# Value blocks side by side behind an undivided fold, scores in the banks they free, and the high parts of a projection ahead of its low parts

## The chip, the cores and the metric

The kernel runs on one core of one Trainium2 chip. The metric is the device time of one execution in microseconds (us). The engines are TensorE (PE; its weight loads are listed apart as PEld), VectorE (DVE), ScalarE (ACT), GpSimd (POOL) and SyncE (SP, which only issues transfers here). PSUM has eight banks of 128 x 512 fp32 numbers, and TensorE writes nowhere else.

## The reference, cut to what matters

```python
h = einsum('bct,bcd->bdt', x, W[condition])          # x: 128 x 32 x 512, W[condition]: 32 x 32
q = (h @ Wq_c.T + bq_c) @ Wq_up.T + bq_up            # 32 heads of 192
kv = h @ Wkv_c.T + bkv_c                             # 64 latent columns, 64 rope columns
k, v = up-projections of the latent columns          # 32 heads of 128
attn = softmax(q k^T / sqrt(192))                    # per batch and head: 32 x 32
x = x + (sum over the heads of attn v) @ Wo.T + bo
x = x + FFN(causal convolution of x along t)         # second half of the kernel, not touched here
```

Each of the 128 batches has a sequence of 32 channels; a feature vector is the 512 time steps.

## The kernel before

The weights are folded so that queries meet the latent columns directly. The attention part works on 8 groups of 16 batches (512 tokens, "tokens" being batch x channel), with 16 of the 32 heads at a time: a *unit* u = 0..15 is one group and one half of the heads, and LAST = 15. Matrices are multiplied as fp32r in three terms, with operands split in a high part (made by a ScalarE copy) and a low part (made by a VectorE subtraction that reads the high part and the source again).

For a unit u of 2 to 14, TensorE's program (lines 916 to 954) does in this order:

- `fold(u, 0, 14)`: for each pair of heads (j, j + 1), 18 matmuls of 64 rows into two PSUM banks, BT and BT + 1 or in turn BS and BS + 1 (line 320). ScalarE copies each head out to `qt` (line 1141), except heads 13 and 15, which VectorE copies (`late_head`, line 1434).
- `values(u - 1, 0)`: 64 small matmuls (32 x 64 tiles, line 807) of the previous unit's probabilities with the latent columns, into the four banks BZ, BZ + 1, BX, BO.
- `fold(u, 14, 16)`: the last pair of heads, into BS and BS + 1.
- `values(u - 1, 1)`: the second value block, into BT, BT + 1, BZ, BZ + 1. It needs the pair in BT copied out, and BZ and BZ + 1 drained of the first block (line 833).
- `scores(u, n)`, n = 0..3, into BS, BS + 1, BX, BT (line 785, 128 x 32 tiles). They need all heads in `qt`; n = 2 and 3 also need a bank of the value blocks drained.
- `output(u - 1, n)`, n = 0..3, twelve matmuls of 128 x 128 for each two of them (lines 628 to 630), accumulated in BO.

To drain a value block is a ScalarE copy `z_high` of each bank (line 1161) and, after each, a VectorE subtraction `z_low` (line 1428), counted by `zl_done`. VectorE then moves the scores from PSUM to `sc` (`take_scores`, line 1407, counted by `s_taken`), and the softmax follows (lines 1409 to 1423), with its exponential `soft` on ScalarE (line 1146).

In an odd unit (u = 1, 3, ..., 13) the next group is projected in between: `output` 0 and 1, then `project`, `output` 2, `mix_features` (line 677), `output` 3. `project` makes four banks of features (n = 0..3, in BS, BS + 1, BT + 1, BT). For each n it runs eight matmuls with the high part of x and then four with the low part (line 636), and tells `feat_ready`. ScalarE first makes the high parts of x (line 1077, when the scores are done), and VectorE makes the low parts after it has taken the scores (line 1374). ScalarE copies each feature bank out in two copies (lines 1081 and 1082), and between these it runs the exponentials of unit u, in the fixed order feat 0, soft 0, feat 1, soft 1, feat 2, soft 2, feat 3 (lines 1271 to 1274). `mix_features` waits for all four (line 670). In units 2 to 5 VectorE also computes some angles for the second half of the kernel, between its softmax and `late_head`.

Engines run their programs in order. Unit 1 has an order of its own: there values(0, 1) comes after two of the four scores.

Of the kernel before, what the change touches and what calls it, by code (L numbers as in the profile page):

```python
# [32 lines left out]
GH = NH // 2  # L33
# [95 lines left out]
def build(nc, d, out):  # L129
# [161 lines left out]
    stored = [mem.sem(f"stored{n}") for n in range(RW)]  # L291

    BT, BS, BZ, BO, BX = 0, 2, 4, 6, 7
    ZBANK = ((BZ, BZ + 1, BX, BO), (BT, BT + 1, BZ, BZ + 1))
    LATE_ZBANK = ((BX, BZ, BZ + 1, BO), (BZ, BZ + 1, BT, BS))
    LAST_ZBANK = ((BT, BT + 1, BS, BS + 1), (BZ, BZ + 1, BX, BT))
    FOLD_BANK = (BT, BS)
    SBANK = (BS, BS + 1, BX, BT)
    FIRST_SBANK = (BT, BX, BS, BS + 1)
    WEIGHT_BANK = (BO, BO, BZ + 1, BO, BZ + 1, BO, BZ + 1, BZ)  # L300
    MIXED_BANK = (BX, BZ + 1, BZ)
# [4 lines left out]
    LAST = NU - 1  # L306
# [4 lines left out]
    FIRST_A = 7  # L311
    BY_DVE_LAST = (C - 3, C - 2, C - 1)
    LATE_TOTAL_BANK = 0
    s_bank = lambda u, n: (FIRST_SBANK if u == 0 else SBANK)[n]
    BY_DVE = (GH - 3, GH - 1)
    qt_count = lambda u, j: GH * u + j - 2 * max(0, min(u, LAST) - 1) - (sum(h < j for h in BY_DVE) if 1 <= u < LAST else 0)
    z_bank = lambda u, m_, b: (LAST_ZBANK if u == LAST else LATE_ZBANK if u == LAST - 1 else ZBANK)[m_][b]
    z_part = lambda tile, m_, b: tile[:, 4 * m_:4 * m_ + 4, :, 32 * b:32 * b + 32].rearrange("p a n c -> p n a c")
    z_made = lambda u, m_, b: ps[:, z_bank(u, m_, b), :].rearrange("p (n a c) -> p n a c", n=4, c=C)
    fold_bank = lambda u, j: FOLD_BANK[j // 2 % 2]  # L320
# [16 lines left out]
    with nc.Block() as block:  # L337
# [288 lines left out]
        def _(pe):  # L626
# [25 lines left out]
            def project(k):  # L652
                u = 2 * k - 1
                for n in range(4):
                    if n != 2:
                        pe.wait_ge(s["s_taken"], 4 * u + (1, 2, 0, 4)[n])
                    else:
                        pe.wait_ge(s["zl_done"], 8 * (u - 1) + 6)
                    for tt in range(TT):
                        if n == 0:  # L660
                            pe.wait_ge(s["xh_done"], 4 * k + tt + 1)
                        projected(k, n, tt, False)
                    for tt in range(TT):
                        if n == 0:
                            pe.wait_ge(s["xl_done"], 4 * k + tt + 1)
                        mm = projected(k, n, tt, True)
                    mm.then_inc(s["feat_ready"], 1)
# [13 lines left out]
            def turn_latent(k):  # L681
                pe.wait_ge(s["kv_done"], k + 1)
                if k == 0:
                    pe.wait_ge(s["mb_done"], 2 * QUADS - 2)
                else:
                    pe.wait_ge(s["zl_done"], 16 * k)
                for g in range(4):
                    mm = pe.transpose(ps[:, BZ + 1, 64 * g:64 * g + 64], kv[0:64, g * P:(g + 1) * P], ident[0:64, 0:64])
                mm.then_inc(s["ct_ready"], 1)
# [81 lines left out]
            def scores(u, n):  # L771
                pe.wait_ge(s["qt_done"], qt_count(u + 1, 0))
                if u >= 1:
                    pe.wait_ge(s["qt_last"], 2 * u)
                if n == 0:
                    pe.wait_ge(s["kv_done"], u // 2 + 1)
                if u == 0 and n == 1:
                    pe.wait_ge(s["q_done"], 1)
                if n == 2 and u >= 1:
                    pe.wait_ge(s["zl_done"], 8 * (u - 1) + 3)  # L780
                if n == 3 and u >= 1:
                    pe.wait_ge(s["zl_done"], 8 * (u - 1) + 5)
                for b in range(4):
                    tok = slice((4 * n + b) * C, (4 * n + b + 1) * C)
                    mm = pe.matmul(ps[32 * b:32 * b + 32, s_bank(u, n), :], kv[:, tok], qt[:, :, tok], start=True, stop=True)  # L785
                mm.then_inc(s["s_ready"], 1)
# [24 lines left out]
            def values(u, m_):  # L811
                v = u + 1
                if m_ == 0:
                    pe.wait_ge(s["ct_done"], u // 2 + 1)
                    pe.wait_ge(s["kv_done"], min(NS, v // 2 + 1))
                    pe.wait_ge(s["q_done"], 2 * min(NS, v // 2 + 1))
                    if u == 0:
                        pe.wait_ge(s["parT_done"], 1)
                        pe.wait_ge(s["mb_done"], 2 * QUADS)
                    else:  # L820
                        pe.wait_ge(s["part_done"], u)
                    if u == 8:
                        pe.wait_ge(s["taps_done"], 2)
                    if u == LAST - 1:
                        pe.wait_ge(s["s_taken"], 4 * LAST + 2)
                else:
                    if v == LAST:
                        pe.wait_ge(s["qt_done"], qt_count(LAST, GH - 1))
                        pe.wait_ge(s["zl_done"], 8 * u + 3)
                    else:  # L830
                        pe.wait_ge(s["qt_done"], qt_count(v, GH - 2))
                        pe.wait_ge(s["qt_last"], 2 * v - 1)
                        pe.wait_ge(s["zl_done"], 8 * u + 2)
                value_block(u, m_, lambda n: 4 * u + n + 1, lambda rows, n, e: pT[rows, n, 8 * m_ + e:8 * m_ + 8:2, :])

            def values_last(h):
# [51 lines left out]

            def tap_products(n):
                pe.wait_ge(s["gf_ready"], 1)  # L890
                if n == 0:
                    pe.wait_ge(s["zl_done"], 64)
                else:
                    pe.wait_ge(s["s_taken"], 4 * 8 + 3)
                for h in range(16 * n, 16 * n + 16):
                    mm = pe.matmul(ps[0:LA, TAP_BANK[n], (h % 16) * LC:(h % 16 + 1) * LC], g_t[:, h, :],
                                   theta[:, h, 2 * LA:NL], start=True, stop=True)
                mm.then_inc(s["taps_ready"], 1)
# [17 lines left out]
            for u in range(1, LAST):  # L916
                if u == 1:
                    fold(u, 0, 8)
                    turn_latent(0)
                    turned_par()  # L920
                    fold(u, 8, 16)
                    values(0, 0)
                    scores(1, 0)
                    scores(1, 1)
                    values(0, 1)
                    scores(1, 2)
                    scores(1, 3)
                else:
                    fold(u, 0, 14)
                    values(u - 1, 0)  # L930
                    fold(u, 14, 16)
                    values(u - 1, 1)
                    for n in range(4):
                        scores(u, n)
# [132 lines left out]
        def _(act):  # L1067
# [162 lines left out]
            for u in range(1, LAST):  # L1230
                if u >= 2:
# [16 lines left out]
                    fold(u, 12, 14)  # L1248
                    if u == LAST - 1:
                        ffn_float(2)  # L1250
                    values(u - 1, 0, 0, 3)
                    fold(u, 14, 16)
                    values(u - 1, 0, 3, 4)
                    if u == 8:
                        decay_exp(3)
                    if u == LAST - 1:
# [103 lines left out]
        def _(dve):  # L1360
# [178 lines left out]
            for u in range(1, LAST):  # L1539
# [15 lines left out]
                    late_head(u, GH - 1)  # L1555
                    values(0, 0, 0, 4)
                else:
                    values(u - 1, 0, 0, 2)
                    late_head(u, GH - 1)
                    values(u - 1, 0, 2, 4)  # L1560
                values(u - 1, 1, 0, 4)
                for n in range(4):
                    take_scores(u, n)
# [198 lines left out]
```

## Time and profile before

| | us |
|---|---|
| median of 3 runs (724.90 to 725.49) | 725.34 |
| the profiled execution, its own time | 725.95 |
| its span in the trace | 724.0 |
| PE busy | 705.0 (97%) |
| DVE busy | 597.2 (82%) |
| ACT busy | 412.6 (57%) |
| POOL busy | 215.3 (30%) |

The granted clock of TensorE is full in all 40 slices of the page. Times in the rows below count from the start of the span. The PE rows give a modelled end, so the start of one row to the start of the next is a truer length than the row's own duration. Consecutive rows of the same engine may overlap for the same reason. A bracket at the end of a row is idle time of that engine before it, and what ended it.

### The profile page before, as it was taken

The numbers are of one execution on the slowest core, as the hardware profiler recorded it, in microseconds if no ns is written. First come the engines' busy times: TensorE is split into PE (matmuls) and PEld (weight loads), VectorE is DVE, ScalarE is ACT, GpSimd is POOL, SyncE is SP. The second block draws the span as 40 slices with busy tenths as digits, with TensorE's granted clock in tenths as the row PEclk, the third lists the DMA queues.
The fourth block names the chain that finished last, engine by engine and source line by source line (L and its number), as shares of the span: only waits on it lengthen the run. The fifth ranks groups of instructions, "written<-read, shape, count | busy, mean of one in ns | idle before, by whom it ended". The sixth has DMA issues, their size and how long they took to land.

```text
span 724.0 us, 17041 instructions
## 1 busy us (share of the span) xinstructions
PE 705.0 (97%) x7154; PEld 567.1 (78%) x7154; DVE 597.2 (82%) x1005; ACT 412.6 (57%) x736; POOL 215.3 (30%) x242
## 2 busy tenths in 40 slices
PE   7999999999999999999999999999999899999997
PEld 6767777787978697878877786978677688888885
DVE  4889999998999678787769776887798689999975
ACT  4676565647556765746565656556664444444443
POOL 5461020020002010550020000003521267777884
PEclk9999999999999999999999999999999999999999
DMA  7900100010002000100100010002112587999942
GB/s 220 329 3 2 51 13 1 2 61 4 1 2 62 3 2 22 39 5 13 60 5 2 2 59 2 1 2 92 60 60 54 139 225 152 181 244 188 239 106 107
DMA packets 31919, 50.94 MB, mean 70 GB/s; under 512 B 6594, under 2 KB 21090, under 8 KB 30562
## 3 DMA queue, kind: packets, MB, share of 16 engines
q1 hardware_dynamic: 29858, 49.26, 25.0%
q8 instruction: 57, 0.93, 0.5%
q0 software_dynamic: 1024, 0.53, 0.4%
q14 instruction: 20, 0.16, 0.1%
q10 hardware_dynamic: 960, 0.06, 0.1%
HBM read 41.19 MB, written 8.63 MB: 69 GB/s over the span
## 4 chain that ended last, share of the span: by engine, by line
PE 76%; DVE 13%; ACT 4%; issue 4%; POOL 2%; DMA 1%; SPq 0%; DVEq 0%; ACTq 0%
PE ps L736 34%; PE ps L785 7%; PE ps L628 5%; PE ps L629 5%; PE ps L630 5%; PE ps L807 4%; PE ps L677 3%; PE ps L636 2%; PE ps L638 2%; PE ps L637 2%; DVE x_low L1663 2%; DVE x_t L1657 2%; DVE y L1701 1%; PE ps L1029 1%; PE ps L1037 1%
## 5 line engine op out<-in xcount | busy, mean ns | idle before, releaser
L1141 ACT ACTIVATE qt<-ps,m_bias 128x512 f32<-128x512 f32 x228 | 145.8, 686 | 87.5 <-PE ps L736 83.9
L736 PE MATMUL ps<-q_high,m_high 64*128 64x512 f32 x768 | 166.0, 397 | 0.2 <-issue 0.2
L736 PE MATMUL ps<-q_high,m_low 64*128 64x512 f32 x768 | 162.4, 388 | 0.2
L736 PE MATMUL ps<-q_low,m_high 64*128 64x512 f32 x768 | 114.4, 387 | 0.0
L736 PEld LDWEIGHTS ps<-q_high,m_high 64*128 64x128 f32 x768 | 89.5, 184 | 15.4 <-issue 5.9
L736 PEld LDWEIGHTS ps<-q_high,m_low 64*128 64x128 f32 x768 | 89.8, 184 | 9.8 <-issue 1.0
L1428 DVE TENSOR_TENSOR z_low<-ps,z_high 128x512 fp32r<-128x512 f32 x128 | 79.8, 681 | 18.7 <-ACT z_high L1161 18.7
L736 PEld LDWEIGHTS ps<-q_low,m_high 64*128 64x128 f32 x768 | 81.6, 184 | 9.8
L1161 ACT CAST z_high<-ps 128x512 fp32r<-128x512 f32 x128 | 66.7, 597 | 14.5 <-PE ps L807 9.9
L1146 ACT ACTIVATE sc<-sc 128x512 f32<-128x512 f32 x60 | 38.1, 634 | 41.5 <-DVE sc L1413 35.2
L494 POOL TENSOR_TENSOR o_sum<-o_part,o_part 128x512 f32<-128x512 f32 x7 | 9.1, 1307 | 173.2 <-ACT o_part L1171 173.2
L459 POOL TENSOR_TENSOR mix<-gathered,block_of 128x256 f32<-128x256 f32 x16 | 10.4, 667 | 161.4 <-PE ps L677 152.1
L785 PE MATMUL ps<-qt,kv 128*32 128x512 f32 x480 | 55.0, 595 | 2.7 <-ACT qt L1141 1.2
L617 POOL TENSOR_TENSOR y_low<-y,y_high 128x512 fp32r<-128x512 f32 x32 | 48.4, 1511 | 18.6 <-ACT y_high L1357 18.5
L628 PE MATMUL ps<-z_high,wvT_high 128*128 128x512 f32 (+1 forms) x132 | 53.6, 406 | 0.0
L1434 DVE TENSOR_SCALAR qt<-ps,m_bias 128x512 f32<-128x512 f32 x28 | 20.9, 750 | 37.7 <-PE ps L736 37.6
L629 PE MATMUL ps<-z_low,wvT_high 128*128 128x512 f32 (+1 forms) x132 | 50.9, 386 | 0.0
L630 PE MATMUL ps<-z_high,wvT_low 128*128 128x512 f32 (+1 forms) x132 | 50.7, 384 | 0.0
L1421 DVE TENSOR_TENSOR sc<-sc,row_stat 128x512 f32<-128x512 f32 x60 | 44.6, 743 | 2.1
L1413 DVE TENSOR_TENSOR sc<-sc,row_stat 128x512 f32<-128x512 f32 x60 | 42.9, 715 | 2.1
L1423 DVE STREAM_TRANSPOSE pT<-sc 128x512 f32<-128x512 f32 x60 | 42.7, 711 | 2.0
L611 POOL TENSOR_TENSOR rest<-rest,x_t 128x512 f32<-128x512 f32 x29 | 37.9, 1308 | 17.0 <-ACT rest L1344 17.0
(259 smaller groups left out, 1468.5 us busy)
## 6 DMA issues: line engine op xcount, KB each, us to landing
x_raw<-in_x_groups SPq DMA_DIRECT2D x32, 256.0 KB
x_t<-in_x_channels SPq DMA_DIRECT2D x8, 1024.0 KB, 7.8
out<-rest SPq DMA_DIRECT2D x32, 256.0 KB, 6.3
toep_high<-taps_scratch SPq DMA_DIRECT2D x32, 192.0 KB, 4.4
toep_low<-taps_scratch SPq DMA_DIRECT2D x32, 192.0 KB, 4.9
w_raw<-in_w_groups SPq DMA_DIRECT2D x8, 512.0 KB, 8.0
toep_far<-taps_scratch SPq DMA_DIRECT2D x32, 64.0 KB, 5.7
rope_raw<-in_rope_rows SPq DMA_DIRECT2D x8, 192.0 KB, 7.7
```

What stands on the lines that cost most here:

```text
L617: pool.tensor_tensor(y_low[g % 2][:, :, ch, :], y[c % 2][:], f(y_high[g % 2][:, :, ch, :]), ALU.subtract).then_inc(s["yl_done"], 1)
L628: pe.matmul(out, lh, rh, start=start, stop=False)
L629: pe.matmul(out, lh, rl, start=False, stop=False)
L630: return pe.matmul(out, ll, rh, start=False, stop=stop)
L736: mm = pe.matmul(ps[:, fold_bank(u, j) + e, :], weights[rows, (GH * g + j) // 2, c, :], moving[c][rows, :], start=start, stop=stop)
L785: mm = pe.matmul(ps[32 * b:32 * b + 32, s_bank(u, n), :], kv[:, tok], qt[:, :, tok], start=True, stop=True)
L1141: act.activation(qt[:, j, :], ps[:, fold_bank(u, j) + j % 2, :], ACT.Identity, bias=m_bias[:, h:h + 1]).then_inc(s["qt_done"], 1)
L1161: act.copy(z_part(z_high, m_, b), z_made(u, m_, b)).then_inc(s["zh_done"], 1)
L1413: dve.tensor_tensor(rows(n), rows(n), wide(n), ALU.subtract).then_inc(s["sub_done"], 1)
L1421: dve.tensor_tensor(rows(n), rows(n), wide(n), ALU.mult).then_inc(s["norm_done"], 1)
L1423: dve.transpose(flat(pT[:, n]), flat(sc[:, n])).then_inc(s["turn_done"], 1)
L1428: dve.tensor_tensor(z_part(z_low, m_, b), z_made(u, m_, b), f(z_part(z_high, m_, b)), ALU.subtract).then_inc(s["zl_done"], 1)
```

## The change

`fold(u, 14, 16)` is run before the first value block, so the fold is undivided and the two value blocks stand side by side. The second block goes to BT, BT + 1, BS, BS + 1 (the banks of the fold) instead of BT, BT + 1, BZ, BZ + 1, and so it waits for all 16 heads to be copied out. The scores of units 2 and up go to BZ, BZ + 1, BX, BT, and each waits for the first, second, third and fifth `z_low`. ScalarE and VectorE take their work in the new order. In `project` the high parts of all four banks come first and the low parts of all four after them; its waits name the new banks. Unit 0's value blocks and unit 1's scores keep their banks, and the last unit keeps its order. Two waits for scores that have been taken are added or renamed (`turn_latent`, `tap_products`), since scores now lie in BZ and BZ + 1.

```diff
-    ZBANK = ((BZ, BZ + 1, BX, BO), (BT, BT + 1, BZ, BZ + 1))
+    FIRST_ZBANK = ((BZ, BZ + 1, BX, BO), (BT, BT + 1, BZ, BZ + 1))
+    ZBANK = ((BZ, BZ + 1, BX, BO), (BT, BT + 1, BS, BS + 1))
-    SBANK = (BS, BS + 1, BX, BT)
+    SECOND_SBANK = (BS, BS + 1, BX, BT)
+    SBANK = (BZ, BZ + 1, BX, BT)
@@ project(k)
                 for n in range(4):
-                    if n != 2:
-                        pe.wait_ge(s["s_taken"], 4 * u + (1, 2, 0, 4)[n])
+                    if u == 1 and n < 2:
+                        pe.wait_ge(s["s_taken"], 4 * u + n + 1)
+                    elif n < 3:
+                        pe.wait_ge(s["zl_done"], 8 * (u - 1) + (7, 8, 6)[n])
                     else:
-                        pe.wait_ge(s["zl_done"], 8 * (u - 1) + 6)
+                        pe.wait_ge(s["s_taken"], 4 * u + 4)
                     for tt in range(TT):
                         if n == 0:
                             pe.wait_ge(s["xh_done"], 4 * k + tt + 1)
                         projected(k, n, tt, False)
+                for n in range(4):
                     for tt in range(TT):
                         if n == 0:
                             pe.wait_ge(s["xl_done"], 4 * k + tt + 1)
@@ turn_latent(k)
                     pe.wait_ge(s["zl_done"], 16 * k)
+                    pe.wait_ge(s["s_taken"], 8 * k + 2)
@@ scores(u, n)
-                if n == 2 and u >= 1:
-                    pe.wait_ge(s["zl_done"], 8 * (u - 1) + 3)
-                if n == 3 and u >= 1:
-                    pe.wait_ge(s["zl_done"], 8 * (u - 1) + 5)
+                if u == 1 and n >= 2:
+                    pe.wait_ge(s["zl_done"], 8 * (u - 1) + 2 * n - 1)
+                if u >= 2:
+                    pe.wait_ge(s["zl_done"], 8 * (u - 1) + (1, 2, 3, 5)[n])
@@ values(u, 1)
-                        pe.wait_ge(s["qt_done"], qt_count(v, GH - 2))
-                        pe.wait_ge(s["qt_last"], 2 * v - 1)
-                        pe.wait_ge(s["zl_done"], 8 * u + 2)
+                        pe.wait_ge(s["qt_done"], qt_count(v + 1, 0))
+                        pe.wait_ge(s["qt_last"], 2 * v)
+                        if u == 0:
+                            pe.wait_ge(s["zl_done"], 8 * u + 2)
@@ tap_products(n)
-                if n == 0:
-                    pe.wait_ge(s["zl_done"], 64)
-                else:
-                    pe.wait_ge(s["s_taken"], 4 * 8 + 3)
+                pe.wait_ge(s["s_taken"], 4 * 8 + (1, 3)[n])
@@ TensorE's order
-                    fold(u, 0, 14)
+                    fold(u, 0, 16)
                     values(u - 1, 0)
-                    fold(u, 14, 16)
                     values(u - 1, 1)
@@ ScalarE's order
-                    values(u - 1, 0, 0, 3)
                     fold(u, 14, 16)
-                    values(u - 1, 0, 3, 4)
+                    values(u - 1, 0, 0, 4)
@@ VectorE's order
-                    values(u - 1, 0, 0, 2)
                     late_head(u, GH - 1)
-                    values(u - 1, 0, 2, 4)
+                    values(u - 1, 0, 0, 4)
```

## Rows read from the trace of the kernel before

**Rows 1.** The page, its parts on busy time and on the chain that ended last.
```profile
PE 705.0 (97%) x7154; PEld 567.1 (78%) x7154; DVE 597.2 (82%) x1005; ACT 412.6 (57%) x736; POOL 215.3 (30%) x242
...
PE 76%; DVE 13%; ACT 4%; issue 4%; POOL 2%; DMA 1%; SPq 0%; DVEq 0%; ACTq 0%
```

**Rows 2.** Stretches: from:to, length, busy PE PEld DVE ACT POOL, clock, DMA share, GB/s.
```profile
92.00:125.00 33.00, 33.00 (x373) 25.29 (x375) 30.65 (x53) 18.77 (x33) 3.82 (x4) 1.00 0.02 3
```

**Rows 3.** Timeline of PE, end of unit 6's fold: start, us, engine, line, operation, shapes.
```profile
237.33 0.84 PE L736 MATMUL ps<-q_low,m_high 64*128 64x512 f32 x6
...
239.37 0.84 PE L736 MATMUL ps<-q_low,m_high 64*128 64x512 f32 x6
240.15 1.21 PE L807 MATMUL ps<-pT,ctok 32*64 32x128 f32 x64
...
243.55 1.20 PE L807 MATMUL ps<-pT,ctok 32*64 32x128 f32 x64
244.68 3.64 PE L785 MATMUL ps<-qt,kv 128*32 128x512 f32 x32
```

**Rows 4.** Timeline of ACT and DVE, same unit: heads 14 and 15, then the scores.
```profile
243.65 0.69 ACT L1141 ACTIVATE qt<-ps,m_bias 128x512 f32<-128x512 f32 x1 [0.69 <-PE ps L736]
...
243.69 0.75 DVE L1434 TENSOR_SCALAR qt<-ps,m_bias 128x512 f32<-128x512 f32 x1 [0.39 <-PE ps L736]
...
247.94 2.50 DVE L1407 STREAM_TRANSPOSE sc<-ps 128x512 f32<-128x512 f32 x4
```

**Rows 5.** Timeline of all engines, unit 1: second value block, its drain, score 3.
```profile
71.58 1.21 PE L807 MATMUL ps<-pT,ctok 32*64 32x128 f32 x64
...
72.83 2.05 ACT L1161 CAST z_high<-ps 128x512 fp32r<-128x512 f32 x4 [1.95 <-PE ps L807]
73.44 1.29 DVE L1428 TENSOR_TENSOR z_low<-ps,z_high 128x512 fp32r<-128x512 f32 x2 [1.43 <-ACT z_high L1161]
...
74.28 0.64 PE L785 MATMUL ps<-qt,kv 128*32 128x512 f32 x4 [0.50 <-DVE z_low L1428]
```

**Rows 6.** Timeline of PE, projection in unit 5: high, low, low, last low, output, mix.
```profile
212.80 0.30 PE L637 MATMUL ps<-wcT_high,x_high 128*128 128x320 f32 x1
...
213.97 1.01 PE L636 MATMUL ps<-wcT_high,x_low 128*128 128x320 f32 x4
...
215.98 0.75 PE L636 MATMUL ps<-wcT_high,x_low 128*128 128x320 f32 x4
...
219.50 0.75 PE L636 MATMUL ps<-wcT_high,x_low 128*128 128x320 f32 x4
220.09 0.39 PE L628 MATMUL ps<-z_high,wvT_high 128*128 128x512 f32 x1
...
221.47 0.38 PE L677 MATMUL ps<-mix,feat 128*128 128x128 f32 x2
```

**Rows 7.** Timeline of ACT: feature copies and exponentials, units 5 and 6.
```profile
216.77 0.43 ACT L1081 COPY feat<-ps 128x320 f32<-128x320 f32 x1 [0.27 <-PE ps L636]
217.09 0.22 ACT L1082 COPY feat<-ps 128x64 f32<-128x64 f32 x1
217.19 0.65 ACT L1146 ACTIVATE sc<-sc 128x512 f32<-128x512 f32 x1
...
229.16 0.63 ACT L1146 ACTIVATE sc<-sc 128x512 f32<-128x512 f32 x1
229.68 0.69 ACT L1103 ACTIVATE kv<-ps,columns 128x512 f32<-128x512 f32 x1
```

**Rows 8.** Timeline of DVE in unit 5: head 13, and the low parts of x.
```profile
202.76 0.75 DVE L1434 TENSOR_SCALAR qt<-ps,m_bias 128x512 f32<-128x512 f32 x1
...
212.06 2.45 DVE L1374 TENSOR_TENSOR x_low<-x_raw,x_high 128x512 fp32r<-128x512 f32 x4
```

**Rows 9.** Timeline of PE, unit 1's projection: its first matmul, and the output after it.
```profile
78.13 0.30 PE L637 MATMUL ps<-wcT_high,x_high 128*128 128x320 f32 x1
...
86.30 0.39 PE L628 MATMUL ps<-z_high,wvT_high 128*128 128x512 f32 x1
```

More of the change, by code:

```diff
@@ L313, in build @@
     LATE_TOTAL_BANK = 0
-    s_bank = lambda u, n: (FIRST_SBANK if u == 0 else SBANK)[n]
+    s_bank = lambda u, n: (FIRST_SBANK if u == 0 else SECOND_SBANK if u == 1 else SBANK)[n]
     BY_DVE = (GH - 3, GH - 1)
     qt_count = lambda u, j: GH * u + j - 2 * max(0, min(u, LAST) - 1) - (sum(h < j for h in BY_DVE) if 1 <= u < LAST else 0)
-    z_bank = lambda u, m_, b: (LAST_ZBANK if u == LAST else LATE_ZBANK if u == LAST - 1 else ZBANK)[m_][b]
+    z_bank = lambda u, m_, b: (LAST_ZBANK if u == LAST else LATE_ZBANK if u == LAST - 1 else FIRST_ZBANK if u == 0 else ZBANK)[m_][b]
     z_part = lambda tile, m_, b: tile[:, 4 * m_:4 * m_ + 4, :, 32 * b:32 * b + 32].rearrange("p a n c -> p n a c")
```

## The prediction

> **What bounds the kernel now.** I read the page first, then the stretches, then the timelines of the engines at the two places that the change touches. TensorE is busy for 97% of the span, and three quarters of the chain that ended last are its own matmuls [rows 1]. Inside the units it has no idle time at all, at full clock, while VectorE has about 2 us free in 33 and ScalarE nearly half its time [rows 2]. So each matmul stream that is shortened, and each new wait of TensorE, goes into the span one for one; work moved on ScalarE or VectorE costs nothing until TensorE waits for it. The change adds and removes no arithmetic. Three things remain to be priced: the switches between fold and value block, the waits in front of blocks and scores, and the waits around the projection.
>
> **The boundary of a unit, before.** Take unit 6 [rows 3]. A pair of heads takes 239.37 - 237.33 = 2.04 us. Its last run of six matmuls starts at 239.37, which I call A. The first value block starts at A + 0.78. A block takes 244.68 - 243.55 = 1.13 us, so between the blocks lie 243.55 - 240.15 - 1.13 = 2.27 us for a pair that takes 2.04 inside an undivided fold. The split therefore costs 0.23 us: one switch of tile shape into the values and one out of them. The scores start at 244.68 = A + 5.31. Unit 6 stands for the rest: the same lengths recur within a few hundredths in nearly all boundaries of units 2 to 13.
>
> **The same boundary after, if nothing waits.** The pair that was in between comes first, so the first block starts at A + 0.78 + 2.04 = A + 2.82, the second at A + 3.95 and the scores at A + 5.08. That is the saving of 0.23.
>
> **The wait in front of the second block.** It now needs heads 14 and 15 copied out. Before, these copies start 0.10 us (ScalarE, 0.69 long) and 0.14 us (VectorE, 0.75 long) after the block behind the fold has started [rows 3, 4]. After the change they end at about A + 2.82 + 0.14 + 0.75 = A + 3.71, plus a signal of 0.1 to 0.2, just before A + 3.95. I take nothing for it. In units 2 to 5 VectorE reaches head 13 late because of the angles (202.76 in unit 5, about a microsecond after that pair was made [rows 8]), and head 15 follows it by 0.7, so the second block may start up to 0.4 late there. What hides this is the next wait.
>
> **The wait in front of the scores.** Score 0 now lies in the bank of the first value block, and it needs that bank drained. Unit 1 shows this very chain, for its score 3: the block starts at 71.58, z_high at 72.83 (1.25 later), z_low at 73.44 (0.61), and the score at 74.28 (0.84), after idle time put down to z_low [rows 5]. That is 2.70 us from the start of a block to a score that needs its first bank. After the change this gives A + 2.82 + 2.70 = A + 5.52, against A + 5.08 if nothing waited and A + 5.31 before. So the stall is 0.44, and the boundary is 0.2 us longer than before, not shorter. The cover that the old order gave was the last pair of heads: the first block was drained under it. The following scores need the second, third and fifth bank. Banks drain every 0.5 to 0.6 us (four z_high in 2.05 [rows 5]) and a score takes 0.9 (a quarter of 3.64 [rows 3]), so they don't wait. There are 13 such boundaries (units 2 to 14): 13 x 0.2 = +2.6 us. The bounds are 13 x -0.23 = -3.0 if the stall were absent, and +5 if ScalarE's conversions of weights, which stand between the two blocks in unit 14, and late copies add as much again.
>
> The trace shows PE losing 0.23 us for the split. The Trainium skill (TensorEngine Tiling, Key Properties) says that a change of the tiling mode drains the array; by that alone the change would gain 3.0 us here and nothing would be set against it. The same page (PSUM Bottleneck) says that after tiling the copies out of PSUM may become the limit, and that speaks against the change; the chain of rows 5 is such a copy.
>
> **The projection, low parts.** VectorE takes the scores, then makes the low parts of x; in unit 5 it does so from 212.06 to 214.51 [rows 8], while TensorE asks for them from 213.97 on. The projection lasts 220.09 - 212.80 = 7.29 us. Its parts are 1.17 for eight high matmuls (213.97 - 212.80) and 0.59 for four low ones (220.09 - 219.50), four of each make 7.04, so TensorE waits 0.25 [rows 6]. In unit 1 the projection takes 86.30 - 78.13 = 8.17 [rows 9], a wait of 1.13. Units 3, 7, 11 and 13 are like unit 5, and unit 9 waits 0.1. With all high parts first, the first low part is wanted 4.68 us after the start, over 2 us after it is there even if VectorE runs a microsecond later. This removes 1.13 + 5 x 0.25 + 0.1 = 2.5 us.
>
> **The projection, feature copies.** Here the change creates a wait. Before, one feature bank is finished every 1.76 us, and ScalarE's copies and exponentials fit between. After it, all four are finished at the very end, 0.59 apart. ScalarE must do, in order, feat 0, soft 0, feat 1, soft 1, feat 2, soft 2, feat 3. One step costs 0.32 + 0.10 for the two copies (216.77, 217.09, 217.19) and 0.54 for an exponential (229.16 to 229.68 is 0.52, and behind a short copy it is 0.02 longer), together 0.96 [rows 7]. That is longer than 0.59, so ScalarE falls behind. Let P be the start of the projection. The low run of bank 0 starts at P + 4.68. Its copy starts 0.79 after the start of the run (216.77 - 215.98 [rows 6, 7]), at P + 5.47. Three steps later, at P + 8.35, comes feat 3, which is complete 0.32 + 0.22 later at P + 8.89, and with a signal of 0.16 TensorE can mix at P + 9.05. Without a wait it would mix at P + 7.04 + (221.47 - 220.09) = P + 8.42 [rows 6]. The stall is 0.63 us, in each of the seven projections: +4.4 us. Its bounds: nothing, if ScalarE should be faster, and 1.0 each if it starts late. Queued behind the waiting mix are output 3 and the next fold; VectorE and ScalarE wait with it for the new queries. The exponentials aren't ready too late: VectorE is through with the first of them 3 us before ScalarE comes to it, even a microsecond later than before.
>
> **The rest.** The waits added to `turn_latent` and `tap_products`, and `project`'s on the new banks, name events at least 1 us old when they are reached; they cost nothing. No transfer is moved, and POOL's and SP's programs are the same. VectorE starts its softmax about 0.8 us later behind each boundary, because two of the eight z_low no longer fit under the fold (it takes the scores at 247.94 = A + 8.57 before [rows 3, 4], and at about A + 9.5 after). It has idle time before head 13 in most units. The last unit's order stays.
>
> **The sum.** +2.6 (boundaries) - 2.5 (low parts) + 4.4 (feature copies) = +4.5 us. The profiled execution took 725.95, so 730.4; the median is 0.6 lower, at 725.34, and from there the forecast is 729.8, that is 0.6% slower.
>
> **Rivals.**
> 1. *No stall at the mix.* If the copies keep up after all, the projection gives its 2.5 us and the boundaries take 2.6: 725.4, no change. For it speaks that ScalarE is half idle [rows 2]. Against it speaks that its idle time lies elsewhere: the order of its program puts three exponentials ahead of feat 3 just then. A stall of half the size gives 727.6 and still belongs to the forecast. Chance 0.10.
> 2. *Faster: the drain is not waited for.* If z_high and z_low of the first bank were done before the scores are reached, the boundaries would give 3.0 us. This decides from the point where the chain from block start to score is under 2.26 us (two blocks) and not 2.70; it needs ScalarE to start on a bank before the whole block is done, which its wait forbids (one signal per block). With the stall at the mix it gives 725.34 - 3.0 - 2.5 + 4.4 = 724.2, and without that too 719.8. The rule of the Trainium skill on draining (TensorEngine Tiling, Key Properties) would show its whole gain in this case; the trace gives it 0.23 us a unit and no more. Chance 0.08 in all.
> 3. *VectorE becomes the bound in the units with angles.* It starts 0.8 us later and was already late in unit 5 [rows 8]. If head 15 or the low parts of the queries are late by 0.5 in units 2 to 5, 2 us come on top: about 732. Against it speak the 0.44 us that the second block has in hand under the wait for the drain. Chance 0.12.
> 4. *Only part of the change acts*, for instance the new bank order runs as computed but the low parts were not what TensorE waited for. Then the 2.5 us are missing: 732.3. The rows put that wait on x_low, so this has 0.03.
>
> **How the numbers follow.** The forecast has the remaining 0.67, with a range of its own of 727.4 to 731.5. The range that should hold the time 8 times in 10 reaches from 726.0 to 732.4. A measurement of this kernel can tell about 0.2%, 1.45 us, from no change. Slower by more than that holds most of the forecast and rivals 3 and 4, 0.78. The same holds rival 1, a bit of the forecast and a bit of rival 2, 0.15. Faster keeps 0.07.
>
> **What would show it.** In the profile after, score 0 of units 2 to 14 should show PE idle of about 0.4 before it, ended by z_low, and score 1 to 3 none. PE idle ended by x_low should be gone from the projection. The first mix matmul should show 0.6 of idle ended by ScalarE's second feature copy, seven times, with ScalarE running without a gap from feat 0 to feat 3. VectorE should take the scores later relative to the fold's end, without anyone waiting for that. It is wrong if the mix starts 1.38 us after the end of the projection as before, or if the scores start right behind the second block.

## The result, and the profile after

| | before | after |
|---|---|---|
| median, us | 725.34 (724.40 to 726.35, 5 runs) | 729.28 (728.59 to 731.06, 5 runs) |
| ratio to before, 95% interval | | 1.0068 (1.0053 to 1.0083) |
| the profiled execution, us | 725.95 | 731.06 |
| its span, us | 724.0 | 729.2 |

The change makes the kernel slower: by 0.7% (4.9 us) by the ratio of the runs, by 3.9 us by the two medians, which lies at the lower end of the ratio's interval. TensorE now has idle time where it had none [rows 2]. The page of the kernel after, its busy times and its last chain, to be held beside [rows 1]:

```profile
PE 702.8 (96%) x7154; PEld 562.1 (77%) x7154; DVE 595.9 (82%) x1005; ACT 408.5 (56%) x736; POOL 213.7 (29%) x242
...
PE 75%; DVE 9%; ACT 8%; issue 4%; POOL 2%; DMA 1%; SPq 0%; DVEq 0%; ACTq 0%
```

ScalarE's share of the chain has gone from 4% to 8%. The waits of the kernel after, PE's own and those of its weight loads, say for what (who waited for whom: us in total, times, longest):

```profile
PE ps L791 <- DVE z_low L1430: 7.5, 15, 0.5
PE ps L682 <- ACT feat L1085: 2.6, 7, 0.4
...
PEld ps L682 <- ACT feat L1085: 5.6, 7, 0.8
PEld ps L742 <- ACT qt L1144: 3.0, 9, 0.4
```

The first is the wait of the scores for the drain: 13 of its 15 times are the boundaries, one is unit 1's, which was there before [rows 5], and one is 0.30 us in front of the last score of unit 14. The second and third are the wait of the mix for the feature copies. Both had been forecast. The last one had not (five of its nine times, 0.4 each). No low part of x is among them: that wait is gone.

**The boundary.** Unit 6 after the change, PE's timeline (beside [rows 3]):

```profile
242.30 0.84 PE L742 MATMUL ps<-q_low,m_high 64*128 64x512 f32 x6
243.07 2.19 PE L813 MATMUL ps<-pT,ctok 32*64 32x128 f32 x128
245.77 3.64 PE L791 MATMUL ps<-qt,kv 128*32 128x512 f32 x32 [0.51 <-DVE z_low L1430]
```

and ScalarE and VectorE there (beside [rows 4]):

```profile
243.18 0.69 ACT L1144 ACTIVATE qt<-ps,m_bias 128x512 f32<-128x512 f32 x1 [1.35 <-PE ps L742]
244.32 4.01 ACT L1164 CAST z_high<-ps 128x512 fp32r<-128x512 f32 x8 [0.45 <-PE ps L813]
...
243.21 0.75 DVE L1436 TENSOR_SCALAR qt<-ps,m_bias 128x512 f32<-128x512 f32 x1 [1.29 <-PE ps L742]
244.94 4.88 DVE L1430 TENSOR_TENSOR z_low<-ps,z_high 128x512 fp32r<-128x512 f32 x8 [0.97 <-ACT z_high L1164]
249.73 2.50 DVE L1409 STREAM_TRANSPOSE sc<-ps 128x512 f32<-128x512 f32 x4
```

The two blocks run as one of 128 matmuls: no wait for heads 14 and 15 between them. From their start to the first score it takes 245.77 - 243.07 = 2.70 us (2.72 in unit 9), and the chain is the one of [rows 5]: z_high after 1.25, z_low 0.62 later, the score 0.83 after that.

**The projection.** Unit 5 after the change, PE and then ScalarE (beside [rows 6, 7]):

```profile
213.31 0.30 PE L639 MATMUL ps<-wcT_high,x_high 128*128 128x320 f32 x1
...
218.00 2.51 PE L638 MATMUL ps<-wcT_high,x_low 128*128 128x320 f32 x16
220.34 0.39 PE L630 MATMUL ps<-z_high,wvT_high 128*128 128x512 f32 x1
...
222.26 2.94 PE L682 MATMUL ps<-mix,feat 128*128 128x128 f32 x24 [0.37 <-ACT feat L1085]
224.96 0.48 PE L630 MATMUL ps<-z_high,wvT_high 128*128 128x512 f32 x1
```

```profile
218.78 0.43 ACT L1084 COPY feat<-ps 128x320 f32<-128x320 f32 x1 [5.97 <-PE ps L638]
219.11 0.22 ACT L1085 COPY feat<-ps 128x64 f32<-128x64 f32 x1
219.21 0.64 ACT L1149 ACTIVATE sc<-sc 128x512 f32<-128x512 f32 x1
219.74 0.43 ACT L1084 COPY feat<-ps 128x320 f32<-128x320 f32 x1
...
221.63 0.46 ACT L1084 COPY feat<-ps 128x320 f32<-128x320 f32 x1
221.93 0.27 ACT L1085 COPY feat<-ps 128x64 f32<-128x64 f32 x1
```

All of it lasts 220.34 - 213.31 = 7.03 us, so the low parts wait for nothing. ScalarE had nothing to do for 6 us and then runs without a gap, 0.96 us for a copy and an exponential. The mix, 1.38 us after the projection if nothing waited, starts at 222.26 instead of 221.72. It also takes 224.96 - 222.26 = 2.70 us up to the next output, where it took 2.60 before the change. Its first weight load starts at 222.26 together with the matmul, where it started 0.22 us ahead of it before.

**The wait that was not forecast.** Start of unit 7's fold after the change, ScalarE and then PEld:

```profile
257.52 0.63 ACT L1149 ACTIVATE sc<-sc 128x512 f32<-128x512 f32 x1 [0.69 <-DVE sc L1415]
258.06 0.35 ACT L1110 COPY ctok<-ps 128x256 f32<-128x256 f32 x1
258.31 2.62 ACT L1144 ACTIVATE qt<-ps,m_bias 128x512 f32<-128x512 f32 x4
...
259.63 0.18 PEld L742 LDWEIGHTS ps<-q_high,m_high 64*128 64x128 f32 x2 [0.43 <-ACT qt L1144]
```

In the even unit ScalarE has one more exponential and the latent copy ahead of the first heads of the next fold. The exponential waits for VectorE, and VectorE starts its softmax later than before: in unit 6 it takes the scores 3.96 us after TensorE starts them, where it was 3.26 [rows 3, 4]. So the first two heads are copied late, and the third pair, which goes into their banks, starts 0.3 us late (259.63, where 258.66 + 0.68 = 259.34 was due).

### The profile page after: what moved, and what is told of

Same layout as the page of the kernel before. It is cut to its first block, busy times and chain, and to the rows that moved or that the text cites. A ratio compares the mean times of both kernels' runs of the same rounds, so it can differ in the third digit from the quotient of the medians.

```text
span 729.2 us, 17041 instructions
## 1 busy us (share of the span) xinstructions
PE 702.8 (96%) x7154; PEld 562.1 (77%) x7154; DVE 595.9 (82%) x1005; ACT 408.5 (56%) x736; POOL 213.7 (29%) x242
## 4 chain that ended last, share of the span: by engine, by line
PE 75%; DVE 9%; ACT 8%; issue 4%; POOL 2%; DMA 1%; SPq 0%; DVEq 0%; ACTq 0%
PE ps L742 36%; PE ps L791 7%; PE ps L630 5%; PE ps L632 5%; PE ps L631 5%; PE ps L682 3%; PE ps L813 3%; PE ps L640 2%; PE ps L639 2%; DVE x_low L1664 2%; DVE x_t L1658 2%; ACT z_high L1164 2%; ACT sc L1149 2%; DVE z_low L1430 2%; DVE y L1702 1%
## 5 line engine op out<-in xcount | busy, mean ns | idle before, releaser
L742 PE MATMUL ps<-q_high,m_high 64*128 64x512 f32 x768 | 157.9, 395 | 0.0
L742 PE MATMUL ps<-q_high,m_low 64*128 64x512 f32 x768 | 154.8, 387 | 0.0
L742 PE MATMUL ps<-q_low,m_high 64*128 64x512 f32 x768 | 110.4, 386 | 0.0
L742 PEld LDWEIGHTS ps<-q_high,m_high 64*128 64x128 f32 x768 | 78.9, 184 | 18.3 <-ACT qt L1144 3.0
L742 PEld LDWEIGHTS ps<-q_high,m_low 64*128 64x128 f32 x768 | 79.0, 184 | 12.1
L742 PEld LDWEIGHTS ps<-q_low,m_high 64*128 64x128 f32 x768 | 75.9, 184 | 12.9
L1164 ACT CAST z_high<-ps 128x512 fp32r<-128x512 f32 x128 | 64.8, 618 | 13.9 <-PE ps L813 9.1
L791 PEld LDWEIGHTS ps<-qt,kv 128*32 128x32 f32 x480 | 16.2, 108 | 37.8 <-issue 34.0
L1423 DVE TENSOR_TENSOR sc<-sc,row_stat 128x512 f32<-128x512 f32 x60 | 43.3, 722 | 2.1
L1415 DVE TENSOR_TENSOR sc<-sc,row_stat 128x512 f32<-128x512 f32 x60 | 42.5, 709 | 2.1
```

The costliest lines, as they stand in the source:

```text
L742: mm = pe.matmul(ps[:, fold_bank(u, j) + e, :], weights[rows, (GH * g + j) // 2, c, :], moving[c][rows, :], start=start, stop=stop)
L1164: act.copy(z_part(z_high, m_, b), z_made(u, m_, b)).then_inc(s["zh_done"], 1)
L1423: dve.tensor_tensor(rows(n), rows(n), wide(n), ALU.mult).then_inc(s["norm_done"], 1)
```

## The experiments

How a run is read beside its time: timelines of PE agree between executions to a few hundredths of a microsecond inside the units, so I take lengths from the starts of the value blocks. Unit 9 is an exception (38.44 us in e4 and 38.56 in e12, the same kernel), and so is unit 2 of e7 and e8, where the granted clock fell (below). An *even unit* is from its first value block to that of the next odd unit, an *odd unit* from there to the next even one (which contains a projection), each the mean of the two that units 10 to 13 have. The *stretch* is from unit 1's second value block to unit 15's first block (the one of `values(LAST - 1, 0)`).

| kernel | even unit | odd unit | stretch | ratio to before, 95% interval |
|---|---|---|---|---|
| before | 28.57 | 38.32 | 468.5 | 1 |
| after | 29.06 | 38.89 | 474.2 | 1.0068 (1.0053 to 1.0083) |
| e1_order_only | 28.57 | 38.70 | 470.0 | 1.0030 (1.0017 to 1.0043) |
| e2_boundary_only | 29.03 | 39.22 | 476.7 | 1.0099 (1.0080 to 1.0118) |
| e3_after_feats_first | 29.02 | 38.25 | 470.7 | 1.0029 (1.0018 to 1.0041) |
| e4_before_high_feats | 28.53 | 38.08 | 466.6 | 0.9971 (0.9958 to 0.9983) |
| e12_e4_again | 28.57 | 38.07 | 466.7 | 0.9979 (0.9969 to 0.9988) |
| e9_e4_angles_shifted | 28.55 | 38.08 | 465.7 | 0.9968 (0.9953 to 0.9983) |
| e5_after_soft3_late | 28.73 | 38.89 | 472.6 | 1.0064 (1.0051 to 1.0077) |
| e6_after_no_low_bank0 | 28.92 | 38.62 | 472.5 | 1.0060 (1.0045 to 1.0075) |
| e11_no_low_soft3 | 28.46 | 38.62 | 469.9 | 1.0021 (1.0008 to 1.0034) |
| e10_after_feats_soft3 | 28.73 | 38.26 | 469.5 | 1.0017 (1.0007 to 1.0028) |
| e8_e4_angles_later | 28.57 | 38.07 | 472.8 | 1.0071 (1.0054 to 1.0087) |
| e7_after_three_orders | 28.73 | 38.27 | 473.5 | 1.0075 (1.0059 to 1.0091) |

### The change in two halves

e1_order_only: the kernel before with the projection's new order alone.

```diff
                         projected(k, n, tt, False)
+                for n in range(4):
                     for tt in range(TT):
```

> The kernel before, with only the projection's order of the change: the high parts of all four feature banks first, then the low parts. The boundaries of the units stay as they were. My theory (the copies of the features finish late because ScalarE has three exponentials between them): the waits for the low parts of x go (-2.5 us in all, read before), and the mix starts about 0.5 us late and takes 0.1 longer in each of seven projections (+4.4 to +5.1), so 725.3 + 1.9 to 2.6, about 727.5. Rival (the whole loss of the changed kernel lies at the boundaries, the new order of the projection is a gain): about 722.8.

726.29 us against 723.81 for the kernel before on that chip, +2.2 us by the ratio. The order alone is a loss: an odd unit grows by 0.38 and an even one not at all. Unit 1, whose wait for the low parts was 1.13, gets 0.5 shorter. The mix waits as in the kernel after:

```profile
PE ps L678 <- ACT feat L1083: 2.6, 7, 0.4
```

e2_boundary_only: the changed kernel with the projection's old order (the line above taken out).

> The changed kernel with the projection's old order (high and low parts bank by bank) and everything else of the change. My theory: +2.6 us for 13 boundaries, +1.5 for fold starts of odd units where ScalarE is late with the first heads, and the low parts of x, which VectorE now makes 0.8 us later, are waited for about 1.0 us instead of 0.25 in six projections (+4.2), with no wait at the mix: about 733.5. Rival (boundaries are worth nothing or gain, and the projection's order is the loss): 725 or under.

731.42 us, +7.2 by the ratio, +8.2 in the stretch. The rival falls. The theory had 733.5, 2 us too much. With the new boundaries the old order of the projection is worse than the new one, because VectorE makes the low parts later and TensorE asks for them at the old moment. The projection takes 7.98 us, which is a wait of 0.94 where it was 0.25:

```profile
PE ps L638 <- DVE x_low L1375: 2.6, 14, 0.2
```

So the two parts of the change belong together, in that the new order hides a wait that the new boundaries would make longer, and each is a loss on the old kernel.

### The mix

e3_after_feats_first: the changed kernel with ScalarE's four feature copies ahead of the exponentials.

```diff
-                    for n in range(3):
-                        feat_taken(i // 2, n)
-                        soft(u, n)
-                    feat_taken(i // 2, 3)
+                    for n in range(4):
+                        feat_taken(i // 2, n)
+                    for n in range(3):
+                        soft(u, n)
```

> The changed kernel, with ScalarE's order in the projection altered: the four feature copies first, then the three exponentials. My theory: feature bank 3 is copied out 7.8 us after the start of the projection, before TensorE comes to the mix at 8.4, so the stall of 0.63 in seven projections goes: -4.4 us, about 724.9. The exponentials still fit before the first query copy. Rival (the mix is late for another reason, the high parts taking longer to reach PSUM or VectorE being late): no change, 729.3.

725.93 us. An odd unit falls from 38.89 to 38.25, which is the 0.63 of the stall, and no wait for a feature copy is left. The total falls by less than expected, 3.4 us in the stretch and not 4.4, because unit 1 gains nothing and unit 5 only 0.2. There the fold now waits for VectorE's part of the queries, which comes behind the angles. Unit 5, PEld and then DVE:

```profile
225.66 0.19 PEld L742 LDWEIGHTS ps<-q_low,m_high 64*128 64x128 f32 x2 [0.52 <-DVE q_low L1393]
```
```profile
222.32 0.80 DVE L1464 TENSOR_SCALAR o_sum<-o_sum 128x512 f32<-128x512 f32 x1
223.29 0.75 DVE L1380 SCALAR_TENSOR_TENSOR q_low<-ps,columns,q_high 128x512 fp32r<-128x512 f32 x1 [0.16 <-DVE o_sum L1464]
```

e4_before_high_feats: the kernel before with both edits, high parts first and feature copies first.

> The kernel before, with the projection's order of the change and ScalarE's four feature copies ahead of the exponentials. The boundaries stay as before. My theory: the waits for low parts go (-2.5 us) and no new one comes: 722.8, which beats both kernels. Rival (late exponentials hold up the softmax, or the high parts cost something by themselves): 725.3 or more.

721.66 us, -2.1 by the ratio, and e12_e4_again is the same kernel measured a second time, on another chip:

> The same kernel as e4_before_high_feats (before, high parts first, four feature copies first), again on another call for a second interval, and as the measure for the run beside it. Theory: ratio to before 0.997, as it was. Rival (the first gain was a draw of the chip): 1.000.

722.13 us, 0.9979. An odd unit falls by 0.25, the wait for the low parts, and an even one stays. Unit 1 gains only 0.4 of its 1.13: its fold now waits 0.8 us (a weight load at 90.67) for VectorE's low parts of the queries, behind the angles. This part of the change is a gain once the copies that follow are put in order. It beats both kernels.

### The late heads

e5_after_soft3_late: in the changed kernel ScalarE's last exponential and latent copy of an even unit come behind heads 0 and 1 of the next fold.

```diff
-                    for n in range(4):
+                    for n in range(3 if u < LAST - 1 else 4):
                         soft(u, n)
-                    if u < LAST - 1:
-                        latent(u // 2)
@@ behind fold(u, 0, 2)
-                    if u % 2 == 0:
-                        soft(u - 1, 3)
+                    soft(u - 1, 3)
+                    if u % 2 == 0:
                         projected_kv(u // 2)
+                    else:
+                        latent((u - 1) // 2)
```

> The changed kernel; ScalarE's last exponential and the latent copy of an even unit come behind the first two heads of the next fold instead of ahead of them. Theory: in five odd units of the changed kernel the third pair of heads starts 0.3 us late, because ScalarE still had the last exponential of VectorE's later softmax ahead of the first heads. That goes, from block to block an even unit takes 28.77 us instead of 29.03, and the time falls by 1.4 to 729.28 - 1.4, about 727.9. Rival (that wait is TensorE's own, or is given back at the next wait): 29.03 and 729.3 as before.

727.88 us, with an even unit at 28.73 instead of 29.06; odd units stay at 38.89. The stretch is 1.6 us shorter. The ratios, 1.0064 and 1.0068, can't tell that from nothing; the lengths can. What is left in an even unit over before, 28.73 - 28.57 = 0.16, is the boundary's own 0.2.

### The drain

e6_after_no_low_bank0: the changed kernel without one subtraction at each boundary (the low part of what lies in that bank keeps an old content).

```diff
                     dve.wait_ge(s["zh_done"], 8 * u + 4 * m_ + b + 1)
+                    if m_ == 0 and b == 0 and 1 <= u < LAST - 1:
+                        dve.sem_inc(s["zl_done"], 1)
+                        continue
```

> The changed kernel without VectorE's subtraction for the first bank of the first value block, in the 13 boundaries of units 2 to 14: the low part of that quarter of the values keeps an old content, and the score that waited for it waits for ScalarE's copy alone. Theory (the drain of the bank is what score 0 waits for): it can start 2.0 us after the block instead of 2.70, so not later than the second block ends at 2.26; the stall of 0.44 goes in 13 boundaries (-5.7), and with VectorE 0.6 us earlier in each unit the late heads at the start of odd units go too (-1.4): about 722.2. Rival (the idle time lies in the switch from values to scores and not in the drain): no more than 1 us faster than 729.3.

727.89 us: the mechanism holds and the size does not. Score 0 now starts right behind the blocks, 2.11 us after their start, so the idle time was the drain and not a switch (in 12 of the 13 boundaries; in unit 9 the second block itself is held up). The ratios, 1.0060 and 1.0068, could not tell this from the rival; the timeline does:

```profile
201.87 2.19 PE L813 MATMUL ps<-pT,ctok 32*64 32x128 f32 x128
203.98 3.93 PE L791 MATMUL ps<-qt,kv 128*32 128x512 f32 x32
```

But the next scores wait in turn (3.93 us instead of 3.64), since the second bank can't be drained earlier than before. The boundary is 0.3 us shorter, not 0.44. And of that an even unit gives back more than half at the next fold (28.92 instead of 29.06), where the third pair now waits 0.56 for ScalarE. Counted from the start of the blocks, the pair starts only 0.1 earlier than without the edit:

```profile
256.90 0.19 PEld L742 LDWEIGHTS ps<-q_high,m_high 64*128 64x128 f32 x2 [0.56 <-ACT qt L1144]
```

e11_no_low_soft3 takes that wait away as well, with the edit of e5.

> The changed kernel without the first bank's subtraction (the low part of that quarter of the values keeps an old content) and with the last exponential and latent copy behind the first two heads. Leaving out the subtraction alone gave 0.3 us at each boundary, and took back a third to a half of it in even units, where the third pair of heads then waited 0.56 us for ScalarE. Theory: with that wait gone too, an even unit takes 28.77 - 0.31 = 28.46 us from block to block (28.91 with the subtraction left out alone), and the stretch from unit 1's second block to the last unit's first is 472.55 - 2.7 = 469.9. Rival (VectorE's softmax sets the pace of even units by itself): 28.7 or more.

725.40 us; an even unit takes 28.46, the stretch 469.9. The two edits give 4.3 us in the stretch together, where either alone gives 1.6: the same microsecond was held by two waits in a row.

### Putting it together

e10_after_feats_soft3: the changed kernel with the edits of e3 and e5.

> The changed kernel with the four feature copies first and the last exponential and latent copy behind the first two heads, VectorE's angles left where they are. Theory: the gains of the two single edits add up: from unit 1's second block to the last unit's first 474.17 - 3.44 - 1.5 = 469.2 us, against 468.5 of the kernel before, so the time is 0 to 0.3% over before. Rival (each relief is given back at the other wait): over 471.

725.00 us, 0.17% over before, stretch 469.5. With both follow-up waits repaired the change costs only its boundaries (13 x 0.2) and what the angles take, less the low parts.

e7_after_three_orders and e8_e4_angles_later try to free unit 1 and 5 of the angles by putting all of them behind the low parts of the queries, the first on top of e10, the second on top of e4.

```diff
-                    angles(*turn)
                     projected_ab(i // 2)
                     projected_ca(i // 2)
                     crossed(i // 2)
+                    angles(*turn)
```

> The changed kernel with three changes of order only: four feature copies ahead of the exponentials, the last exponential and latent copy behind the first two heads, and VectorE's angles of odd units behind the low parts of the queries. Theory: it keeps the +2.6 us of the boundaries and the -2.5 of the low parts, has no stall at the mix, no late heads, and no fold that waits for VectorE's query parts in units 1 and 5 (which took back 0.7 and 0.4 us when only the feature copies were moved): about 725, equal to the kernel before. Rival (the boundary's loss is more than 0.2 us once the rest is gone): over 727.

> The kernel before with the projection's high parts first, four feature copies first, and VectorE's angles of odd units behind the low parts of the queries. The last of the three should give back what unit 1 lost to the angles: 0.7 us off the kernel without it (721.66), about 721.0; from the second value block of unit 1 to the first of unit 2 33.7 us instead of 34.37. Rival (the low parts of the queries were not late): 34.37 and 721.7.

729.27 and 728.54 us, so both theories failed. Unit 1 gains its 0.7 (33.64 us to unit 2's first block in e8), but VectorE, which had done the angles while it waited for the mix, now does them at the expense of what follows, and is late with head 13 in units 2 and 4. The second value block of unit 2 waits 3.2 us (e8, VectorE's timeline and then PE's):

```profile
107.45 0.69 DVE L1444 SCALAR_TENSOR_TENSOR o_sum<-o_sum,quarter 128x512 f32<-128x512 f32 x1
108.18 0.75 DVE L1435 TENSOR_SCALAR qt<-ps,m_bias 128x512 f32<-128x512 f32 x1
108.85 1.28 DVE L1429 TENSOR_TENSOR z_low<-ps,z_high 128x512 fp32r<-128x512 f32 x2
```
```profile
110.38 1.20 PE L808 MATMUL ps<-pT,ctok 32*64 32x128 f32 x64 [3.21 <-DVE z_low L1429]
```

In unit 4 that block comes 2.1 us late. The two waits are not all of the loss. From unit 2 to unit 3 e8 takes 33.50 us instead of 28.57, and 3.27 of these 4.93 are the wait. The rest is TensorE's clock, which was granted at the lower of its levels for 3.4 us behind the wait (stretches of e8: from:to, length, busy PE PEld DVE ACT POOL, clock, DMA share, GB/s):

```profile
108.00:110.00 2.00, 0.00 (x0) 0.00 (x0) 1.97 (x4) 0.37 (x1) 0.00 (x0) 1.00 0.00 0
110.00:112.00 2.00, 1.62 (x68) 1.14 (x72) 1.98 (x4) 0.38 (x1) 0.00 (x0) 0.92 0.00 0
112.00:114.00 2.00, 2.00 (x16) 0.51 (x12) 1.76 (x3) 1.67 (x4) 0.00 (x0) 0.50 0.00 0
114.00:116.00 2.00, 2.00 (x20) 0.62 (x16) 1.94 (x4) 0.00 (x0) 0.00 (x0) 0.72 0.04 8
```

The missing shares of these rows, (0.08 + 0.50 + 0.28) x 2 = 1.7 us, are what the lower clock cost. The profile of e7 has the same fall, for 3.4 us from 110.0 on, behind an idle time of 2.74 us in front of unit 2's second block. Over their whole length the executions of e7 had a mean granted clock of 1.000 (727.07 us), 0.998 (728.18 and 728.93) and 0.994 (729.61 to 730.42), so part of its miss is the clock and part the lateness. The number of e7's rival, over 727, came true, but not its cause: the boundaries of units 10 to 14 are as long as in e10.

e9_e4_angles_shifted moves three of the 48 steps to unit 6 instead, two out of unit 1's projection and one out of unit 5's.

```diff
                 if u == 2:
-                    angles(7, 14)
+                    angles(5, 12)
...
+                if u == 6:
+                    angles(45, 48)
-                        turn = {1: (0, 7), 3: (21, 27), 5: (41, 48)}.get(u, (0, 0))
+                        turn = {1: (0, 5), 3: (19, 25), 5: (39, 45)}.get(u, (0, 0))
```

> e4_before_high_feats with two of VectorE's 48 angle steps moved out of the gap of unit 1's projection, each later share beginning two steps earlier, and the last three steps done at the start of unit 6, where VectorE has 4 us free. Theory: unit 1's fold no longer waits 0.8 us for the low parts of the queries, from the second value block of unit 1 to the first of unit 2 it takes 33.6 us instead of 34.37, and the time is 0.7 us under the same kernel without the shift. Rival (the shift only moves VectorE's lateness to units 2 and 4, as putting all the angles behind the queries did): no gain, or slower.

721.62 us, 0.9968, with 33.64 us in unit 1 instead of 34.33. The stretch is 465.7, the shortest of all; the 0.7 us beside e12 (722.13, measured along with it) shows in the timeline, and the times alone could not tell it.

## Why the prediction was right, point by point

The forecast was 729.8 and slower; the median is 729.28. The stretch, in which all that the change touches lies but for the last unit, has grown by 474.2 - 468.5 = 5.7 us, where the sum said 4.5; the ratio gives 3.8 to 6.0. That the median comes within 0.5 of the forecast is partly luck. In the stretch the sum is 1.2 short, because it lacks a term of 1.5 (below), and the medians of five executions each, in which what lies ahead of the stretch varies by more than a microsecond, differ by only 3.9.

- *The boundary, +0.2 in each of 13.* Right in ten of them and in the sum. From block to score 2.70 us, as taken from unit 1; e5 leaves 0.16 in an even unit when the late heads are gone. From the start of the seventh pair of heads to the first output, e5 is longer than before by 0.17 to 0.20 in ten boundaries, by 0.37 in unit 8 and by 0.32 in unit 14 (whose last score waits, within the bounds given), and shorter by 0.23 in unit 9, where the old second block had a wait of 0.38 of its own: 2.4 us together, against 2.6. Without the wait the scores would come 2.11 after the start of the blocks (e6), not 2.26: two blocks behind each other are 0.15 shorter than twice the length that I took, so the stall is 0.59 and not 0.44. That changes no sum, since the drain sets the moment. The Trainium skill (TensorEngine Tiling (Array Packing), Key Properties) says that a change of tiling mode drains the array. The 0.15 us fit a loss of that kind; no run here shows that the array is drained. The Trainium skill (the same page, PSUM Bottleneck) warns that copies out of PSUM may become the limit. The 0.59 that the scores wait bears this out.
- *The second block waits for nothing.* Right, in all 13 boundaries: the second block starts 0.99 to 1.00 us after the first.
- *The low parts, -2.5.* Right. e4 shows 0.25 in an odd unit.
- *The feature copies, +0.63 in each of seven.* Right, as 0.54 of wait and 0.10 of a mix that starts without its weights loaded; e3 gives back 0.63 to 0.66 in units without angles.
- *"VectorE should take the scores later ..., without anyone waiting for that."* This is the step that failed. I priced VectorE's 0.8 us by VectorE's own idle time and did not follow who stands behind it: ScalarE's last exponential and latent copy wait for it, and the first heads of an odd unit's fold wait in ScalarE's queue behind these. That costs 0.3 in each of five odd units, 1.5 us (e5), and with it the sum is 6.0, against 5.7 in the stretch.
- *Unit 1 and the angles.* The stall at the mix covered a second lateness, of VectorE's angles. It did not show in the sum and cost nothing, but it took back 1 us of e3's gain.
- The profiled execution of after has 1.8 us over the median of its runs. Before unit 1 the granted clock of TensorE was for 3.4 us at the lower of its two levels, which it was not in the profile of before (last section); by those rows that cost (0.46 + 0.39) x 2 = 1.7 us. It lies outside the stretch. What lies ahead of the stretch differs by up to 2.5 us between the profiles here (unit 1's second block starts at 69.04 in e4 and at 71.58 in before), so single executions differ by that too.

## What to carry to other kernels

When work is moved together, the engines that empty it get it in one lump. Take the length from the producer's start to the bank being free again from any place in the trace where it is bare, and see whether the consumer comes sooner than that; here the saved switches (0.23 to 0.38 us a boundary) were worth less than the 0.59 of that wait. And follow a delayed engine past its own idle time, to the engine that queues behind it: its in-order program carries the delay to work that has nothing to do with it. A wait that is repaired is worth its full length only if no second one stands right behind it, and lengths between marks in the timeline show that to a few hundredths where times of whole runs can't.

## What the runs showed of the hardware that was not expected

Two value blocks behind each other take 2.11 us where two apart take 2 x 1.13. The wait in front of the 24 matmuls of the mix cost 0.1 us more than its length (2.70 against 2.60), and their first weight load was held back with them. In the profile of after, the granted clock of TensorE was 0.54 from 16 to 18 us, so nearly all of that at the lower of its two levels, 1.2 GHz, and 0.61 in the two us after it; in the profile of before it was full. From 12 to 14 us TensorE was busy 0.92 us in the one and 1.41 in the other, from 14 to 16 us 1.40 and 0.97, so over the four the two are alike (stretches of the kernel after: from:to, length, busy PE PEld DVE ACT POOL, clock, DMA share, GB/s):

```profile
12.00:14.00 2.00, 0.92 (x7) 0.65 (x5) 1.15 (x4) 0.59 (x3) 0.62 (x1) 1.00 0.29 55
14.00:16.00 2.00, 1.40 (x35) 1.39 (x36) 0.39 (x2) 1.06 (x4) 1.33 (x8) 1.00 0.26 60
16.00:18.00 2.00, 2.00 (x13) 2.00 (x12) 1.04 (x4) 0.87 (x2) 1.70 (x2) 0.54 0.92 337
18.00:20.00 2.00, 2.00 (x13) 2.00 (x12) 1.03 (x2) 1.01 (x3) 1.39 (x3) 0.61 0.83 271
```

In that gap TensorE waits for a first load (`bq_n`), 1.7 us in after, 1.6 in before, and 1.4 (e3) to 2.2 (e1) elsewhere. The same fall, for 3.4 us, stands in the profile of e2 at 14.7 us, and in those of e7 and e8 in unit 2. There TensorE had been busy 0.62 and 0.64 us (e7, from 106 to 108 and from 108 to 110) and 1.17 and 0.00 us (e8, the same stretches). In unit 4 of e8 it was busy 0.74 and 1.23 us (from 178 to 182), and the clock stayed full. So idle times of TensorE of 1.7 us (after), 2.1 (e2), 2.7 (e7) and 3.2 (e8) went with a loss of 1.7 us beside their own length, and others of 1.6 us (before), 2.0 (e8, unit 4) and 2.2 (e1) did not. What decides it was not tried.
